# Attention by pairs of row tiles: transposed scores of one group beside plain scores of the next

## The reference, cut to what matters

```python
q = _split_heads(query @ Wq.T + bq)
k = _split_heads(key @ Wk.T + bk)
v = _split_heads(value @ Wv.T + bv)
score = jnp.einsum('bhqd,bhkd->bhqk', q, k) * SCALE
attn = jax.nn.softmax(score, axis=-1)
out = jnp.einsum('bhqk,bhkd->bhqd', attn, v)
out = out.transpose(0, 2, 1, 3).reshape(query.shape[0], query.shape[1], D)
return out @ Wp.T + bp
```

## Time and profile before

| | us |
|---|---|
| median of 3 runs (lowest, highest) | 1269.1 (1262.51, 1280.69) |
| the profiled execution | 1263.41 |
| its span, first to last instruction | 1261.6 |
| PE, DVE, ACT, POOL busy in the span | 1035.9, 721.5, 529.5, 557.5 |

### The profile page before, as it was taken

How to read it: one execution, slowest core, us unless ns; L and a number is a source line. 1 busy time by engine, 2 the same in 40 slices (tenths; PEclk the granted TensorE clock), 3 DMA queues, 4 the chain that set the end, 5 groups by cost and what they waited for, 6 DMA issues and landing times. The chain is left out here.

```text
span 1261.6 us, 26409 instructions
## 1 busy us (share of the span) xinstructions
PE 1035.9 (82%) x10017; PEld 744.4 (59%) x10017; DVE 721.5 (57%) x2205; ACT 529.5 (42%) x816; POOL 557.5 (44%) x602
## 2 busy tenths in 40 slices
PE   5715888665787757999992689899999989989998
PEld 1203666543555535666661467788888778856665
DVE  6662778975565653877773544444444545425554
ACT  2435988642333324666662223332332425223222
POOL 4203899866565661555556644443333521001110
PEclk9957999977888878999995555655555769669999
DMA  8323111051111121333322101111100311013331
GB/s 263 138 60 81 33 39 42 11 181 47 41 42 41 43 101 59 118 127 120 124 94 60 34 24 29 32 32 29 35 27 27 90 27 36 19 35 99 91 92 42
DMA packets 65613, 84.03 MB, mean 67 GB/s; under 512 B 18800, under 2 KB 40368, under 8 KB 64720
## 3 DMA queue, kind: packets, MB, share of 16 engines
q1 hardware_dynamic: 53360, 64.64, 16.8%
q0 software_dynamic: 8192, 16.79, 4.6%
q10 hardware_dynamic: 3936, 0.92, 0.4%
HBM read 51.64 MB, written 30.67 MB: 65 GB/s over the span
## 5 line engine op out<-in xcount | busy, mean ns | idle before, releaser
L1766 DVE TENSOR_REDUCE split_table<-attn_psN 128x16 f32<-128x1024 f32 x62 | 75.9, 1224 | 161.1 <-PE attn_psN L1563 157.1
L1563 PE MATMUL attn_psN<-attn_keys,attn_queries 32*128 32x128 f32 x992 | 139.4, 414 | 21.4 <-DMA early_ctxT<-in_ctxT 10.2
L1708 ACT ACTIVATE split_table<-attn_psT 128x2048 f32<-128x2048 f32 x32 | 60.1, 1877 | 200.3 <-PE attn_psT L1584 200.3
L1563 PEld LDWEIGHTS attn_psN<-attn_keys,attn_queries 32*128 32x128 f32 x992 | 108.4, 287 | 56.1 <-issue 36.4
L1030 POOL TENSOR_TENSOR moe_h_lo<-moe_hid,moe_h_hi 128x512 f16<-128x512 f32 x78 | 90.6, 1162 | 101.0 <-ACT moe_h_hi L1185 96.1
L1597 PEld LDWEIGHTS attn_psO<-heads_vheads,split_table 128*64 128x64 f32 x2048 | 102.7, 204 | 13.8 <-issue 9.1
L1597 PE MATMUL attn_psO<-heads_vheads,split_table 128*64 128x18 f32 x2048 | 109.4, 259 | 0.0
L1282 DVE SCALAR_TENSOR_TENSOR moe_hid<-moe_psU,split_to_hidden,moe_act_g 128x512 f32<-128x512 f32 x110 | 81.0, 748 | 36.8 <-ACT moe_act_g L1179 36.7
L1580 PE MATMUL attn_psT<-attn_queries,attn_keys 32*128 32x128 f32 x1024 | 91.9, 440 | 4.4 <-DVE attn_shift L1782 4.1
L1179 ACT ACTIVATE moe_act_g<-moe_psG,split_unscale 128x512 f32<-128x512 f32 x110 | 75.6, 688 | 45.4 <-PE moe_psU L1114 34.5
L1580 PEld LDWEIGHTS attn_psT<-attn_queries,attn_keys 32*128 32x128 f32 x1024 | 79.4, 297 | 9.6 <-DVE attn_shift L1782 7.7
(11 more groups left out here) (266 smaller groups left out, 2694.1 us busy)
## 6 DMA issues: line engine op xcount, KB each, us to landing
scratch_ys<-cell_h SPq DMA_DIRECT2D x26, 256.0 KB, 2.0
res_x<-in_x SPq DMA_DIRECT2D x16, 256.0 KB, 6.2
early_ctxT<-in_ctxT SPq DMA_DIRECT2D x16, 256.0 KB, 6.3
mlstm_packed<-in_values SPq DMA_DIRECT2D x16, 256.0 KB, 2.7
scratch_x<-split_table SPq DMA_DIRECT2D x16, 256.0 KB, 2.3
ffn_x<-scratch_x SPq DMA_DIRECT2D x32, 128.0 KB, 2.8
out<-raw_keys SPq DMA_DIRECT2D x32, 128.0 KB, 2.3
cell_xn<-scratch_xs SPq DMA_DIRECT2D x14, 256.0 KB, 2.6
```

Of the source, the lines that this page charges most:

```text
L1563: ins = pe.matmul(bank[:, at:at + P], queries[g % 3][rows, b, :, :].rearrange("p n t -> p (n t)"), keys[g % 3][rows, b, :, :].rearrange("p ...
L1708: act.activation(probT[half][:, :, :, :].rearrange("p r b q -> p (r b q)"), psT[:, :], ACT.Exp).then_inc(prob_done, 1)
L1766: v.tensor_reduce(peak[:, :, 2 * i:2 * i + 2, :], plain_bank(g, i).rearrange("p (r b m t) -> p r b m t", r=HR, b=2, m=HM), AX.X, ALU.max). ...
```

## The change

The attention's rounds consist of four phases (half of the samples, pair of row tiles). In a phase one pair of row tiles does the transposed scores of four samples of group g, and the other pair the plain scores of the same four samples of group g+1. psT shrinks to two banks, and the exponential is taken four times a group; psO is doubled, turn_heads and project get a bank psB, and turn_peak goes to psF. `values` are cut in halves that stand between the phases; `half_plain` is gone; ScalarE copies the keys after the queries; `out_` stands ahead of `shift_out`. In the routing phase the values of a group are projected by 4 products of 128 columns, copied to a stage, and brought to their place by four DMAs from ScalarE's queue. Some constants share room (ident, bias, parts, shift, past).

```diff
             def project_v(g):
                 pe.wait_ge(k_raw, ONE + g + 1)
-                for b in range(GB):
-                    at = (g * GB + b) * S
-                    for half in range(2):
-                        ins = pe.matmul(psKV[half * S:(half + 1) * S, b * S:(b + 1) * S], given.ctxT[:, at:at + S],
-                                        given.wv[:, half * S:(half + 1) * S], start=True, stop=True)
+                for t in range(TILES):
+                    at = (g + 1) * GROUP + t * P
+                    ins = pe.matmul(psKV[:, t * P:(t + 1) * P], given.ctxT[:, at:at + P], given.wv[:, :], start=True, stop=True)
                 ins.then_inc(v_full, 1)
...
             def v_out(g):
+                staged, final = (given.ctxT[:, n * GROUP:(n + 1) * GROUP].rearrange("p (t n c) -> p t n c", t=TILES, n=2) for n in (g + 1, g))
                 act.wait_ge(v_full, ONE + g + 1)
-                act.activation(given.ctxT[:, g * GROUP:(g + 1) * GROUP], psKV[:, :], ACT.Copy).then_inc(v_raw, 1)
+                act.activation(given.ctxT[:, (g + 1) * GROUP:(g + 2) * GROUP], psKV[:, :], ACT.Copy).then_inc(v_raw, 1)
+                act.wait_ge(v_raw, ONE + g + 1)
+                act.wait_ge(v_moved, ONE + 16 * 4 * g)
+                for b2 in range(2):
+                    for half in range(2):
+                        act.dma_start(final[half * S:(half + 1) * S, :, b2, :], staged[b2 * S:(b2 + 1) * S, :, half, :]).then_inc(v_moved, 16)
...
-        psN, psT = r.ps("psN", [P, 2 * 512]), r.ps("psT", [P, HR * 512])
-        psO, psF = r.ps("psO", [P, 512]), r.ps("psF", [P, 512])
+        psN, psT = r.ps("psN", [P, 2 * 512]), r.ps("psT", [P, 2 * 512])
+        psO, psF, psB = [r.ps(f"psO{c}", [P, 512]) for c in range(2)], r.ps("psF", [P, 512]), r.ps("psB", [P, 512])
...
+        PHASES = tuple((half, pair) for half in range(2) for pair in range(2))
...
+        def row_tiles(pair):
+
+            return [(k, slice((2 * pair + k) * RH, (2 * pair + k + 1) * RH)) for k in range(2)]
...
+            def ready_for_plain(g, n):
+                pe.wait_ge(q_done, ONE + g + 1)
+                pe.wait_ge(k_done, ONE + g + 1)
+                pe.wait_ge(peak_done, ONE + (4 * g + n if g else max(n - 1, 0)))
+
+            def plain(g, n, bl):
+                half, pair = PHASES[n]
+                b = 2 * HALF * half + bl
+                for k, rows in row_tiles(1 - pair):
+                    at = k * 512 + bl * P
+                    ins = pe.matmul(plain_bank(g, n)[:, at:at + P], queries[g % 3][rows, b, :, :].rearrange("p n t -> p (n t)"),
+                                    keys[g % 3][rows, b, :, :].rearrange("p m t -> p (m t)"), start=True, stop=True)
+                if bl == 2 * HALF - 1:
+                    ins.then_inc(plain_done, 1)
...
+            def both_scores(g, n):
+                half, pair = PHASES[n]
+                now, one = there(g), there(g + 1)
+                if one:
+                    ready_for_plain(g + 1, n)
+                if now:
+                    pe.wait_ge(prob_done, ONE + 4 * g + n)
                 for bl in range(2 * HALF):
                     b = 2 * HALF * half + bl
...
+                    if now:
+                        for k, rows in row_tiles(pair):
+                            at = k * 512 + bl * P
+                            pe.matmul(psT[:, at:at + P], keys[g % 3][rows, b, :, :].rearrange("p m t -> p (m t)"),
+                                      queries[g % 3][rows, b, :, :].rearrange("p n t -> p (n t)"), start=True, stop=False)
+                    if one:
+                        plain(g + 1, n, bl)
+                    if now:
+                        if bl == 0:
+                            pe.wait_ge(shift_done, ONE + g + 1)
+                        for k, rows in row_tiles(pair):
+                            at = k * 512 + bl * P
+                            ins = pe.matmul(psT[:, at:at + P], sel[rows, b, :], shift[rows, :], start=False, stop=True)
+                if now:
+                    ins.then_inc(scores_done, 1)
...
+                both_scores(g, 0)
                 if two:
                     turn(g + 2)
                 if was:
                     values(g - 1, 2)
...
+                both_scores(g, 1)
                 if was:
-                    values(g - 1, 3)
...
+                    values(g - 1, 3, (0,))
                 if two:
                     q_(g + 2)
...
+                both_scores(g, 2)
+                if was:
+                    values(g - 1, 3, (1,))
                 if now:
-                    values(g, 0)
+                    values(g, 0, (0,))
                 if was:
                     turn_heads(g - 1)
...
+                both_scores(g, 3)
                 if now:
-                    values(g, 1)
+                    values(g, 0, (1,))
                 if was:
                     project(g - 1)
+                if now:
+                    values(g, 1, (0,))
                 if one:
                     turn_peak(g + 1)
+                if now:
+                    values(g, 1, (1,))
...
+            def probs(g, n):
+                half, pair = PHASES[n]
+                act.wait_ge(scores_done, ONE + 4 * g + n + 1)
+                if g:
+                    act.wait_ge(values_done, ONE + 2 * g + half - 1)
+                act.activation(probT[half][:, 2 * pair:2 * pair + 2, :, :].rearrange("p r b q -> p (r b q)"), psT[:, :],
+                               ACT.Exp).then_inc(prob_done, 1)
...
                 if two:
                     xnT_out(g + 2)
-                    k_out(g + 2)
                 if now:
                     probs(g, 1)
                 if two:
                     q_out(g + 2)
+                    k_out(g + 2)
+                if now:
+                    probs(g, 2)
                 if was:
                     headsT_out(g - 1)
+                if now:
+                    probs(g, 3)
...
                     split_peak(g + 1)
+                if was:
+                    out_(g - 1)
+                if one:
                     shift_out(g + 1)
                 if now:
                     heads_out(g, 0)
-                if was:
-                    out_(g - 1)
```

More of the change, by code:

```diff
@@ L951, in phase_moe @@
         hid = [[r.sb(f"hid{u}{c}", [P, GROUP]) for c in range(CH0)] for u in range(2)]
+        past, past_tiles = (hid[0][c][:, 0:SLOT_TILES * E0].rearrange("p (j e) -> p j e", e=E0) for c in range(2))
+        full = past_tiles[:, 0:GROUPS, :].rearrange("p g e -> p e g")
         h_hi = [[r.sb(f"h_hi{u}{c}", [P, GROUP], F16) for c in range(CH0)] for u in range(3)]
@@ L1576, in scores @@
                 for bl in range(2 * HALF):
                     b = 2 * HALF * half + bl
-                    for rr in range(HR):
-                        rows, at = slice(rr * RH, (rr + 1) * RH), rr * 512 + bl * P
-                        pe.matmul(psT[:, at:at + P], keys[g % 3][rows, b, :, :].rearrange("p m t -> p (m t)"),
-                                  queries[g % 3][rows, b, :, :].rearrange("p n t -> p (n t)"), start=True, stop=False)
-                    for rr in range(HR):
-                        rows, at = slice(rr * RH, (rr + 1) * RH), rr * 512 + bl * P
-                        ins = pe.matmul(psT[:, at:at + P], sel[rows, b, :], shift[rows, :], start=False, stop=True)
@@ L1588, in values @@
+                    if now:
[6 more added lines that the diff above has]
+                    ins.then_inc(scores_done, 1)
+            def values(g, i, parts=(0, 1)):
                 half, il = i // HALF, i % HALF
-                n_ = 2 * g + half
@@ L1590, in values @@
[L1590 removed]
+                pe.wait_ge(prob_done, ONE + 4 * g + 2 * half + 2)
                 pe.wait_ge(v_done, ONE + g + 1)
[L1592 to L1593 removed]
+                if g:
+                    pe.wait_ge(heads_done, ONE + 2 * g + half - 1)
+                for at in range(HP1 // 2 * parts[0], HP1 // 2 * (parts[-1] + 1)):
                     rr, n = at // HN, at % HN
@@ L1629, in _ @@
                 now, one, two, was = there(g), there(g + 1), there(g + 2), there(g - 1)
-                if one:
-                    plain(g + 1, 0, 0)
-                if now:
-                    scores(g, 0)
-                if one:
-                    plain(g + 1, 0, 1)
+                both_scores(g, 0)
                 if two:
```

162 lines of the change are left out of this document (58 added, 104 removed).

## The result

| | before | changed |
|---|---|---|
| median of four runs, us (lowest, highest) | 1266.4 (1262.5, 1280.7) | 1287.0 (1282.6, 1299.0) |
| profiled execution: span, granted clock | 1261.6, 0.785 | 1289.0, 0.754 |

The changed kernel is slower: 1.0125 of the time before, 95% interval 1.0068 to 1.0182 (an estimate from the fast runs alone; the quotient of the two medians is 1.016). The forecast was 1264, "no change", with an own range of 1250 to 1282. The slowdown is under the 2% that the forecast called the least to be told apart, and yet clear of the noise; the time lies above that range.

What follows compares the result with a forecast made beforehand. TensorE's own work at its granted clock was taken to bound the attention phase. From 1263.4 us, -7, -3, +5.3 and +2.2 gave 1261; set between that and the median of 1269.1, the forecast was 1264, range 1250 to 1282.

Steps and rivals of the forecast that it cites:

- The hold: Groups with gathers: signal after values held until 5.8 us from first gather, phase 3 delayed, +2.8 us a group at 0.50.
- Rival "no hold": Groups with gathers: the signal after half the values passes, phase 3 does not wait; 1227 us, chance 0.22.
- The saving: Attention at clock 0.5: four phases take 10.8 us in place of 14.2, -3.4 us a group.
- the 14.2 us: Attention group of the kernel before: scores and plain scores, what remains of the 27.70 us period.
- the forecast's -7: Twelve groups with gathers: -3.4 saved plus 2.8 of wait in each, -7 us in sum.
- The late groups: Three groups without gathers before the last: about -0.9 us each at clock 1.0, -3 us in sum.
- the rival "slower": Groups without gathers lose clock 1.0 through a 1 us wait, 24.3 in place of 14.6 us each; 1293 us, chance 0.15.
- The clock as a rival: Attention: all four tiles used in every phase, more groups granted clock 1.0; 1187 us, chance 0.08.
- Last group: Attention's last group: four phases of two tiles replace two calls of four, +5.3 us at clock 0.5.
- Routing: Routing phase: four DMA issues ahead of tanh, less some 0.5 for shorter products, +2.2 us.
- Pairs run side by side: Attention phases: plain scores lie under a 2.63 us scores call; the rival, one after the other, 1305 us, chance 0.05.

Runs made afterwards that it cites:

- e2: Changed kernel with the gathers of groups 4 to 15 left out: 1242.0 us (1199.4 to 1265.9).
- e1: Kernel before with the gathers of groups 4 to 15 left out: 1145.8 us, 0.896 of the kernel before.
- e5: Changed kernel without the gathers of groups 4 to 15, values no longer cut ahead of phase 3: 1131.7 us, 0.898 of the kernel before.
- e7: Kernel before without the gathers of groups 4 to 15, heads_out(g-1,1) moved behind maximum 2 and normalise on VectorE: 1255.7 us, 0.989 of the kernel before.
- e10: e6 with the gathers issued two at a time behind each maximum: 1212.8 us, 0.943 of the kernel before.
- e15: Kernel before with each gather of groups 4 to 15 replaced by a GpSimd subtraction: 1220.8 us, 0.947 of the kernel before.
- e6: Changed kernel with gathers, values grouped as in e5, last group's scores in all four row tiles: 1251.1 us, 0.983 of the kernel before.

## Why the prediction was wrong, step by step

**The hold: right in size, partly by luck.** It forecast phase 3 to start 11.3 us after the end of phase 1. Measured: 895.59 - 884.20 = 11.4. Two errors cancel in it: the first gather came 4.3 us after that end and not 3.5, since the statistics ended at 886.73, 0.7 later than estimated; and the release came 4.91 us after it and not 5.8. Without gathers (e2) phase 3 starts 848.76 - 839.73 = 9.0 us after, against 8.5 forecast. Rival "no hold" is out. Two readings around it were too narrow. The hold was tied to streams of values, and phase 2's scores were held as well. And it was said to cost the kernel before nothing at clock 0.50; e1 puts it at 0.8 us a group.

**The saving: mis-sized.** 3.4 us a group was forecast at 0.50; e2 shows 27.71 - 25.34 = 2.4, and 0.8 of these are the gathers' absence, so the phases alone save 1.6; the 14.2 us that the forecast set against them held these 0.8. Phases last 2.76 us and not 2.7 (11.0 for four); values in halves take 7.7 us in all and not 7.32; and 0.3 us pass in waits around turn_heads. A miss of 1 us a group is 12 us over twelve groups, more than the whole of the forecast's -7. That the measured period with gathers is again 27.7, and not 28.1 (25.34 plus 2.8), is due to a short stretch at clock 1.0 that the round shown has right after q_, ahead of the standstill (its phase 2 takes 2.39 us and not 2.76). Over the first ten periods the changed kernel still gained 8.9 us (271.5 against 280.4), 8.3 of it in one group at a clock of 0.85 (19.40 us); in which groups an execution gets 1.0 is chance as far as the runs show.

**The late groups: the step that failed.** The forecast took -3 for the three groups without gathers: it let them keep the clock 1.0 and priced their new wait at its own 1 us. They took 25.33 + 24.34 + 23.04 = 72.7 us against 17.45 + 15.47 + 20.67 = 53.6: +19.1. This is the rival "slower" (chance 0.15, 1293 us, measured 1287), with the mechanism it named, the wait ahead of phase 3 behind heads_out and the maximum: 1 us by estimate, 1.12 at 1082.55 and 1083.88 in the changed kernel and 1.13 in e2. That 1287 came so near its 1293 is in part luck: it had +29 for these groups, since only one of the three ran at 1.0 throughout before, and the two periods ahead of them, where the kernel before had a stretch at 1.0, added +7. Two of the three groups (periods 25.33 and 23.04) were at 0.50 from end to end; why the clock did not rise in them stays open, but where it did rise it fell at these waits, and with the waits and the gathers gone (e5) it stayed up for twelve groups. What misled me was to give each wait its own length as a price. At clock 1.0 a group costs 15 us and at 0.50 it costs 25, so a wait of 1 us that ends a stretch at 1.0 costs some ten times its length for each group that follows. The fall behind 3.03 us was before me, and I weighed it as a rival only.

**The clock as a rival: right on its condition.** 14.6 us a group at 1.0 were forecast, e5 shows 14.75; it needed an order without standstills and an absence of gathers that the change did not bring. Rows 1 seemed to say that a busy TensorE does not rise; e1 says what rows 1 couldn't: once up, the kernel before stays up for 124 us if nothing stops it. The Trainium skill's advice ("TensorE: Matmul & The Clock Gate", section "Why this matters for your kernels") to leave no gaps agrees with e1, e5 and e7; I had set it aside over rows 1. The gaps that it warns of are longer than the waits of e2, e10 and e15, and here the measurement decides: the clock fell behind those too.

**Last group**: +6.5 against +5.3: four phases of 2.76 in place of two calls of 2.77 are 5.5, the rest is waits. e6 takes 5.3 of it back. **Routing**: +1.7 in the profiles, +2.2 forecast, not separable from the spread. **Pairs run side by side**: right; a phase takes 2.76 us at 0.50 and 1.47 at 1.0.

## What to carry to other kernels

Where TensorE's granted clock has two levels, first ask what keeps the kernel at the lower one, and price a new wait by the stretch at full clock that it can end, not by its length. Test it by leaving out the suspected cause altogether: e1 showed 134.5 us in a kernel whose TensorE was 99% busy in its attention, a price that no sum of busy time or waits gave. When a round is cut into more, shorter phases with single buffers between them, keep work of one kind together where it covers the copies out of those buffers, and look at where other engines' bursts fall.

## What I had not expected of the hardware

The gathers of the kernel before cost 134.5 us of 1280, though TensorE never waits for their data: eight indirect DMAs a group, about 1.2 us each on GpSimd, hold TensorE's signals back by up to 3.5 us, and a hold that makes TensorE stand can take the clock from 1.0 to 0.50; at 0.50 they still cost 0.8 us a group. With ordinary DMAs of the same size at the same places the time was 0.904 of the kernel before, with none 0.896. And GpSimd arithmetic beside VectorE's normalise made that 3.5 times as long (3.88 us against 1.11).
